# An attention layer and an RWKV block in one pipeline: mixing products in pairs of row groups, additions moved to VectorE, and the FFN shift made on ScalarE

## The reference, cut to what matters

```
def _block(x, state, ...):
    xa = _ln(x, ln1_w, ln1_b)
    sx = concatenate([state[:, 1:2] - xa[:, :1], xa[:, :-1] - xa[:, 1:]], axis=1)
    xxx = tanh((xa + sx * maa_x) @ maa_w1).reshape(b, l, 5, DM)      # DM = 32
    xxx = einsum('blfd,fde->blfe', xxx, maa_w2)
    xm = xa[:, :, None] + sx[:, :, None] * (maa_stack + xxx)
    xk, xw, xv, xr, xg = (xm[:, :, j] for j in range(5))
    w = exp(-exp(time_decay + tanh(xw @ td_w1) @ td_w2))             # DD = 64
    r, k, v = xr @ Wr.T, xk @ Wk.T, xv @ Wv.T
    g = silu(xg @ Wg.T)
    # recurrence over time, per head of 16:  out = r.(u*k v + s);  s = k v + w*s
    og = group_norm(out) * gn_w + gn_b
    x1 = x + og * g @ Wo.T
    xc = _ln(x1, ln2_w, ln2_b)
    sx2 = concatenate([state[:, 0:1] - xc[:, :1], xc[:, :-1] - xc[:, 1:]], axis=1)
    xk2 = xc + sx2 * ffn_maa_k
    xr2 = xc + sx2 * ffn_maa_r
    return x1 + sigmoid(xr2 @ Wfr.T) * (square(relu(xk2 @ Wfk.T)) @ Wfv.T)
```

## Time and profile before

| | |
|---|---|
| median of 3 runs | 2310.33 us (2305.45 to 2311.19) |
| the profiled execution | 2308.37 us |
| its span, first to last instruction | 2306.2 us |
| mean granted TensorE clock | 0.953 |
| HBM traffic | 77 GB/s over the span |

### The profile page before, as it was taken

How to read it: one execution, slowest core, us unless ns; L and a number is a source line. 1 busy time by engine, 2 the same in 40 slices (tenths; PEclk the granted TensorE clock), 3 DMA queues, 4 the chain that set the end, 5 groups by cost and what they waited for, 6 DMA issues and landing times. The chain is left out here.

```text
span 2306.2 us, 34734 instructions
## 1 busy us (share of the span) xinstructions
PE 1971.5 (85%) x12548; PEld 1364.5 (59%) x12548; DVE 1993.5 (86%) x2788; ACT 904.6 (39%) x1793; POOL 1118.4 (48%) x818
## 2 busy tenths in 40 slices
PE   6778898889898889899889889888889888999746
PEld 3556665556666556666555666555666555666624
DVE  3698899988999898899898989998898998899872
ACT  3334434344433443434444443434443334444111
POOL 1344555454555554455545455545455555445431
PEclk8999999999999999999999999999999999999877
DMA  5232232222232232232222223222223222222220
GB/s 199 76 86 83 79 88 78 82 78 81 83 91 79 80 83 79 78 89 78 82 81 79 85 82 88 79 81 77 83 82 87 80 81 83 76 76 81 78 60 9
DMA packets 86136, 189.17 MB, mean 82 GB/s; under 512 B 18800, under 2 KB 35312, under 8 KB 84944
## 3 DMA queue, kind: packets, MB, share of 16 engines
q1 hardware_dynamic: 64464, 170.19, 25.8%
q10 hardware_dynamic: 21504, 16.78, 2.4%
HBM read 161.78 MB, written 16.78 MB: 77 GB/s over the span
## 5 line engine op out<-in xcount | busy, mean ns | idle before, releaser
L605 DVE TENSOR_TENSOR_SCAN S<-wrep,S 128x1024 f32<-128x1024 f32 x256 | 605.8, 2366 | 3.4
L430 POOL TENSOR_TENSOR xf<-xf,xa 128x512 f32<-128x512 f32 x160 | 321.9, 2012 | 285.5 <-DVE xf L570 281.1
L446 POOL COPY S<-s 128x8 f32<-128x8 f32 x256 | 283.5, 1108 | 310.2 <-PE bank L1071 276.7
L614 DVE TENSOR_TENSOR S<-S,rT 128x1024 f32<-128x1024 f32 x256 | 363.3, 1419 | 3.4
L596 DVE TENSOR_TENSOR S<-vrep,kT 128x1016 f32<-128x1016 f32 x256 | 341.5, 1334 | 0.0
L400 POOL TENSOR_SCALAR rstd<-mv 128x1 f32<-128x1 f32 (+1 forms) x96 | 102.3, 1066 | 489.5 <-DVE mv L534 302.1
L1071 PE MATMUL bank<-S,slide 128*32 128x256 f32 x2048 | 176.1, 418 | 130.5 <-DVE S L614 130.5
L570 DVE SCALAR_TENSOR_TENSOR xf<-bank,par,sx 128x128 f32<-128x128 f32 x640 | 179.1, 341 | 59.2 <-PE bank L1031 56.4
L957 PE MATMUL bank<-xf,Wk 128*128 128x128 f32 x1024 | 128.4, 286 | 66.9 <-ACT prob L778 63.6
L402 POOL TENSOR_TENSOR hrs<-hrs,mhalf 128x32 f32<-128x32 f32 x32 | 175.5, 5486 | 2.7
L1071 PEld LDWEIGHTS bank<-S,slide 128*32 128x32 f32 x2048 | 41.5, 111 | 224.0 <-DVE S L614 161.7
(11 more groups left out here) (124 smaller groups left out, 3607.1 us busy)
## 6 DMA issues: line engine op xcount, KB each, us to landing
vrep<-v_dram SPq DMA_DIRECT2D x256, 512.0 KB
xc<-x_c SPq DMA_DIRECT2D x32, 256.0 KB, 2.6
xs<-x_s SPq DMA_DIRECT2D x32, 256.0 KB, 3.0
xres<-xin SPq DMA_DIRECT2D x32, 256.0 KB, 2.4
v_dram<-vT ACTq DMA_DIRECT2D x32, 256.0 KB, 2.3
out<-rr ACTq DMA_DIRECT2D x32, 256.0 KB, 2.9
Wv<-big_w SPq DMA_DIRECT2D x1, 1024.0 KB, 8.2
Wk<-big_w SPq DMA_DIRECT2D x1, 1024.0 KB, 10.0
```

The source lines that it names most:

```text
L430: po.tensor_tensor(xf[:, b, :, :], xf[:, b, :, :], xa[:, :, 1:P + 1], ALU.add).then_inc(pool_mid.sem, 1)
L446: po.tensor_copy(S[:, u % 2, :, 0], s0[:, p, k:k + UJ]).then_inc(pool_wkv.sem, 1)
L605: ve_.tensor_tensor_scan(s, wrep[:, u % C, :, :].rearrange("p j t -> p (j t)"), s, 0.0, ALU.mult, ALU.add).then_inc(dve_wkv.sem, 1)
L614: ve_.tensor_tensor(s, s, rT[:, p, u % C, :].unsqueeze(1).broadcast_to([P, UJ, P]), ALU.mult).then_inc(dve_wkv.sem, 1)
```

## The change

Three edits at once.

1. Mixing products in pairs. `mid_M` takes two factors and alternates between them, so that neighbouring products use different groups of 32 rows and different banks: `v` with `w`, `k` with `r`; `g` stays alone. `Mr` moves ahead of `Vp`. The decay's second product is made in two groups of 64 rows as well: `D1` now makes its result twice (128 columns of weights rather than 64), and `D2` and a new job `E2` share the four chunks. The lists of banks change with it: `Vp` takes the bank of `S2`, `D1` that of `S3`, `Kp` that of `Mk`.
2. The additions of `xa` to `xf` and the last residual addition go from GpSimd to VectorE, each right behind the instructions that it needs. The mixing of `r` moves from behind outer product 5 to ahead of read 4 on VectorE.
3. The FFN shift as two halves: GpSimd computes from the parameters, once, `prev` = ln2 * mix and `here` = ln2 - prev; ScalarE makes from the transposed row, in 16 activations, `xk2` and `xr2` with `here` and `xp2` (one column later) with `prev`; VectorE adds the two with one instruction for each of `xk2` and `xr2`. All eight activations for `xk2` come before those for `xr2`.

```
-    "Tx:mid Mn:att Mm:att V:att W1:mid S0:att S1:att Mv:mid Mw:mid S2:att S3:att Mk:mid Vp:mid D1:mid "
-    "Kp:mid Mr:mid D2:mid T0:att T1:att T2:att T3:att Mg:mid Rp:mid O:att G:mid").split())]
+    "Tx:mid Mn:att Mm:att V:att W1:mid S0:att S1:att Mv:mid Mw:mid S2:att S3:att Mk:mid Mr:mid Vp:mid "
+    "D1:mid Kp:mid D2:mid E2:mid T0:att T1:att T2:att T3:att Mg:mid Rp:mid O:att G:mid").split())]
...
# GpSimd, once
+            ln = par[:, COLS["ln2_w"]:COLS["ln2_w"] + 2 * C].rearrange("p (k c) -> p k c", k=2)
+            for i, name in enumerate(("ffn_maa_k", "ffn_maa_r")):
+                mix = par[:, COLS[name]:COLS[name] + C].unsqueeze(1).broadcast_to([P, 2, C])
+                po.tensor_tensor(prev[:, i, :, :], ln, mix, ALU.mult).then_inc(pool_const, 1)
+            eng.wait_ge(pool_const, 12)
+            for i in range(2):
+                po.tensor_tensor(here[:, i, :, :], ln, prev[:, i, :, :], ALU.subtract).then_inc(pool_const, 1)
...
# GpSimd, each step
-            def mid_add(n, m, p, i):
-                f, b = ORDER[i], i % 3
-                eng.wait_ge(dve_mid.sem, dve_mid.count(f"m{f}", n))
-                po.tensor_tensor(xf[:, b, :, :], xf[:, b, :, :], xa[:, :, 1:P + 1],
-                                 ALU.add).then_inc(pool_mid.sem, 1)
...
-                po.tensor_copy(xc2[:, :, 0], st0[:, p, :]).then_inc(pool_tail.sem, 1)
-            def fin_out(n, m, p):
-                eng.wait_ge(dve_fin.sem, dve_fin.count("y", n))
-                po.tensor_tensor(rr[:, :], rr[:, :], x1[:, :], ALU.add).then_inc(pool_fin.sem, 1)
+                po.tensor_tensor(xp2[:, :, :, 0], st0[:, p, :].unsqueeze(1).broadcast_to([P, 2, C]), mix,
+                                 ALU.mult).then_inc(pool_tail.sem, 1)
...
# VectorE, mid_mix
                 last.then_inc(dve_mid.sem, 1)
+                eng.wait_ge(dve_mid.sem, dve_mid.count(f"m{f}", n))
+                ve_.tensor_tensor(xf[:, b, :, :], xf[:, b, :, :], xa[:, :, 1:P + 1],
+                                  ALU.add).then_inc(dve_mid.sem, 1)
...
# VectorE, tail_shift becomes tail_mix
-                ve_.tensor_tensor(sx2[:, :, :], xc2[:, :, 0:P], xc2[:, :, 1:P + 1],
-                                  ALU.subtract).then_inc(dve_tail.sem, 1)
...
-                for dst, mix in ((xk2, "ffn_maa_k"), (xr2, "ffn_maa_r")):
-                    for c in range(C):
-                        last = ve_.scalar_tensor_tensor(dst[:, c, :], sx2[:, c, :], col(mix, c), xc2[:, c, 1:P + 1],
-                                                        ALU.mult, ALU.add)
-                    last.then_inc(dve_tail.sem, 1)
+                for i, (dst, label) in enumerate(((xk2, "xk"), (xr2, "xr"))):
+                    eng.wait_ge(act_tail.sem, act_tail.count(label, n))
+                    ve_.tensor_tensor(dst[:, :, :], dst[:, :, :], xp2[:, i, :, 0:P], ALU.add).then_inc(dve_tail.sem, 1)
...
# VectorE, fin_y
+                eng.wait_ge(dve_fin.sem, dve_fin.count("y", n))
+                ve_.tensor_tensor(rr[:, :], rr[:, :], x1[:, :], ALU.add).then_inc(dve_fin.sem, 1)
...
# ScalarE, tail_xc2
-                for c in range(C):
-                    last = sc.activation(xc2[:, c, 1:P + 1], bank_of("Tx2")[:, c * P:(c + 1) * P], ACT.Identity,
-                                         bias=col("ln2_b", c), scale=col("ln2_w", c))
-                last.then_inc(act_tail.sem, 1)
+                eng.wait_ge(pe_fin.sem, pe_fin.count("FR", n - 1))
+                for i, dst in enumerate((xk2, xr2)):
+                    for c in range(C):
+                        ps = bank_of("Tx2")[:, c * P:(c + 1) * P]
+                        sc.activation(dst[:, c, :], ps, ACT.Identity,
+                                      bias=here[:, i, 1, c:c + 1], scale=here[:, i, 0, c:c + 1])
+                        last = sc.activation(xp2[:, i, c, 1:P + 1], ps, ACT.Identity,
+                                             bias=prev[:, i, 1, c:c + 1], scale=prev[:, i, 0, c:c + 1])
+                    last.then_inc(act_tail.sem, 1)
...
# TensorE, mid_M
+            def mid_M(n, m, p, fs):
+                eng.wait_ge(act_mid.sem, act_mid.count("tx", n))
+                for f in fs:
+                    eng.wait_ge(*bank_free(f"M{f}", n))
+                for c in range(C):
+                    for f in fs:
+                        i = MIX.index(f)
+                        w, x_ = (w2g[:, :], txg[:, :]) if f == "g" else \
+                            (w2[DM * i:DM * i + DM, :], tx[DM * i:DM * i + DM, :])
+                        last = pe.matmul(bank_of(f"M{f}")[:, c * P:(c + 1) * P], w[:, c * P:(c + 1) * P], x_,
+                                         start=True, stop=True)
+                        if c == C - 1:
+                            last.then_inc(pe_mid.sem, 1)
...
# TensorE, mid_D2
-                for c in range(C):
-                    last = pe.matmul(bank_of("D2")[:, c * P:(c + 1) * P], tw2[:, c * P:(c + 1) * P], dt[:, :],
+                eng.wait_ge(*bank_free("E2", n))
+                for c in range(2):
+                    pe.matmul(bank_of("D2")[:, c * P:(c + 1) * P], tw2[0:DD, c, :], dt[0:DD, :],
+                              start=True, stop=True)
+                    last = pe.matmul(bank_of("E2")[:, c * P:(c + 1) * P], tw2[DD:P, c, :], dt[DD:P, :],
                                      start=True, stop=True)
...
# TensorE, the order of a step
-                if m: mid_M(*m, "v")
+                if m: mid_M(*m, "vw")
                 if w: wkv_sum(*w, 2)
-                if m: mid_M(*m, "w")
                 if a: att_S(*a, 2)
                 if a: att_S(*a, 3)
-                if m: mid_M(*m, "k")
+                if m: mid_M(*m, "kr")
                 if t: tail_Tg(*t)
                 if m: mid_P(*m, "v", "Vp", "Wv")
                 if w: wkv_sum(*w, 3)
                 if m: mid_D1(*m)
                 if m: mid_P(*m, "k", "Kp", "Wk")
-                if m: mid_M(*m, "r")
```

More of the change, by code:

```diff
@@ L31 @@
 U = C * HS // UJ
-CONSTS = 10 + C
+CONSTS = 14 + C
 LAG = {"att": 0, "mid": 1, "wkv": 2, "tail": 3, "fin": 4}
@@ L118, in build @@
         gnh = sb("gnh", [P, 2, C])
+        here = sb("here", [P, 2, 2, C])
+        prev = sb("prev", [P, 2, 2, C])
         W = {name: sb(name, [P, C, E]) for name in BIG}
@@ L175, in build @@
         nmr2 = sb("nmr2", [P, 1])
-        xc2 = sb("xc2", [P, C, P + 1])
-        sx2 = sb("sx2", [P, C, P])
+        xp2 = sb("xp2", [P, 2, C, P + 1])
         xr2 = sb("xr2", [P, C, P])
@@ L217, in build @@
         dve_att = Steps(sem("dve_att"), "stats aggr nm mx0 mx1 ri0 ri1 mx2 mx3 ri2 ri3 xin xst xag nm1")
-        dve_mid = Steps(sem("dve_mid"), "sx xx mv mw mk mr mg g s0m s0c")
+        dve_mid = Steps(sem("dve_mid"), "sx xx mv fv mw fw mk fk mr fr mg fg g s0m s0c")
         dve_wkv = Steps(sem("dve_wkv"), units("a s q"))
-        dve_tail = Steps(sem("dve_tail"), "o1 var o3 og x1 st ag nm sx2 xk2 xr2")
-        dve_fin = Steps(sem("dve_fin"), "y")
+        dve_tail = Steps(sem("dve_tail"), "o1 var o3 og x1 st ag nm xk2 xr2")
+        dve_fin = Steps(sem("dve_fin"), "y out")
         act_att = Steps(sem("act_att"), "xn yn Mn Mm v p0 p1 n0 n1 p2 p3 n2 n3 T0 T1 T2 T3 xhat")
@@ L224, in build @@
         act_decay = Steps(sem("act_decay"), "w0 w1 w2 w3")
-        act_tail = Steps(sem("act_tail"), "o4 sq oT xh xc2")
+        act_tail = Steps(sem("act_tail"), "o4 sq oT xh xk xr")
         act_fin = Steps(sem("act_fin"), "kr kk thr rr")
         pool_att = Steps(sem("pool_att"), "ve rs ve1 rs1")
-        pool_mid = Steps(sem("pool_mid"), "xa0 fv fw fk fr fg")
+        pool_mid = Steps(sem("pool_mid"), "xa0")
         pool_wkv = Steps(sem("pool_wkv"), "z0 z1 rk z2 z3 z4 z5 z6 z7")
         pool_tail = Steps(sem("pool_tail"), "hve hrs ve rs xc20")
-        pool_fin = Steps(sem("pool_fin"), "out")
         pe_att = Steps(sem("pe_att"), "Mn Mm V S0 S1 S2 S3 T0 T1 T2 T3 O")
-        pe_mid = Steps(sem("pe_mid"), "Tx W1 Mv Mw Mk Vp D1 Kp Mr D2 Mg Rp G")
+        pe_mid = Steps(sem("pe_mid"), "Tx W1 Mv Mw Mk Mr Vp D1 Kp D2 Mg Rp G")
         pe_wkv = Steps(sem("pe_wkv"), units("r"))
@@ L817, in mid_dt @@
                 eng.wait_ge(pe_mid.sem, pe_mid.count("D1", n))
-                sc.activation(dt[:, :], bank_of("D1")[0:DD, 0:P], ACT.Tanh).then_inc(act_mid.sem, 1)
+                sc.activation(dt[:, :], bank_of("D1")[:, 0:P], ACT.Tanh).then_inc(act_mid.sem, 1)
             def mid_k(n, m, p):
@@ L828, in mid_ez @@
                 for c in range(C):
-                    last = sc.activation(ez[:, c, :], bank_of("D2")[:, c * P:(c + 1) * P], ACT.Exp,
+                    ps = bank_of("D2" if c < 2 else "E2")
+                    last = sc.activation(ez[:, c, :], ps[:, c % 2 * P:(c % 2 + 1) * P], ACT.Exp,
                                          bias=col("time_decay", c))
@@ L896, in fin_store @@
             def fin_store(n, m, p):
-                eng.wait_ge(pool_fin.sem, pool_fin.count("out", n))
+                eng.wait_ge(dve_fin.sem, dve_fin.count("out", n))
```

55 lines of the change are left out of this document (18 added, 37 removed).

## The result

The changed kernel takes 2393.26 us (median of 4 runs, 2391.82 to 2393.61), the kernel before 2309.84 (4 runs, 2305.45 to 2311.19): a ratio of 1.0369, 95% interval 1.0354 to 1.0384, so slower by 3.7%. The predicted 2375 was 18 us short; the measured time lies inside the prediction's range of 2308 to 2412, and 0.3 us above the upper end of the forecast's own, 2353 to 2393. The profiled run took 2393.61, with a span of 2391.9 and a mean granted clock of 0.916; before, the span was 2306.2 and the clock 0.953.

A forecast was written before the change was run, and what follows sets the result against it. Two loops of near-equal length: VectorE's own work, and its maxima through ScalarE and TensorE to its FFN shift. The latter gave 70.63 us a step: 2.2 over 29 steps, plus 4, made 2378, leaned to 2375 us; range 2308 to 2412.

The forecast's parts named there:

- Steps 1 and 2: Two additions delay max2 and its exponential to m + 8.88; Vp, on S2's bank, starts at 9.81, not 6.41.
- Step 3: ScalarE in order: vT 3.78 us after Vp's start, two DMA issues 1.55 more, so tile 3's exponential starts at 15.14.
- Step 4: On TensorE, D1 takes S3's bank and starts at m + 16.07, where Kp started at 13.91.
- Step 5: TensorE from D1 to Tx2: 17.18 us without a gap, 0.10 less for split D2; Tx2 starts at m + 33.15.
- Step 6: ScalarE starts 1.63 us after Tx2; sixteen activations 0.347 apart take 5.66, ending at m + 40.44.
- Step 7: VectorE's last shift addition follows ScalarE, the read 0.65 later at m + 41.09; about 2.2 us of waiting.
- Row groups: Paired mixing products on TensorE: loads mostly one after another, so Mv 0.5 us later at m; split D2 0.1 less.
- row groups run together: Rival: TensorE's row groups do overlap; step 69.6 us, total 2349; chance 0.12.
- the clock once more: Rival: TensorE's granted clock falls a second time, at Vp; 1.2 us taken, step 71.8, total 2412; chance 0.09.
- VectorE's own sum: VectorE's work per step: 4.26 added, 1.56 removed, 3.26 of GpSimd hold-ups given back; net -0.56 us.
- The clock falls in no step: Rival: TensorE's once-a-step clock fall at the head sum's gap never comes; step 69.0 us, total 2332; chance 0.12.
- VectorE's balance decides: Rival: ScalarE's xr is ready by m + 38.2, so VectorE's work sets the step, 67.86; about 2298; chance 0.16.

The follow-up runs named there:

- a_fill: The changed kernel with unread products in TensorE's four gaps (before the first head sum, S3, Vp and D1): 2293.16 us, ratio 0.9929 to the kernel before.
- p2_fill_all: `p2_only` with unread products in all its gaps (before the first head sum, S3, Vp and Kp): 2306.38 us, ratio 1.0015 to the kernel before.
- a_fill_S3: The changed kernel with two unread products in the gap before S3 only: 2396.27 us, ratio 1.0379 to the kernel before.
- p2_fill: `p2_only` with unread products before the first head sum (three) and before Kp (two): 2371.66 us, ratio 1.0265 to the kernel before.
- p2_only: The kernel before with only the additions moved from GpSimd to VectorE, old lists of banks: 2394.2 us, ratio 1.0374.
- max2_early: The changed kernel with VectorE's reciprocal 1 and maximum 2 ahead of scan 3: 2330.8 us, ratio 1.0088 to the kernel before.
- p3_only: The kernel before with only the FFN shift made in two halves: 2303.97 us, ratio 0.999.

## Why the prediction was right, and where it was not

The direction, the place and the range were right; the forecast's step of 70.63 was 0.9 to 1.1 short, as the net of a term that was left out of the sum and two that were taken too high. The ordinary step of 71.49 us, against the prediction's own steps:

- *Steps 1 and 2.* `Vp` starts at m + 9.82 (1181.11); predicted 9.81. The exponential of S2 releases it.
- *Step 3.* vT follows the start of `Vp` by 5.57 us, not 3.78, since `Vp` runs at the lower clock. The two DMA issues end with the start of exp3, at m + 16.99 instead of 15.14.
- *Step 4.* `D1` starts at m + 17.91 (1189.20) instead of 16.07. **This 1.84 is the size that was missing**, and nearly all of it is the clock: a second fall was a rival with a chance of 0.09 and a price of 1.2.
- *Step 5.* From `D1` to `Tx2` are 16.55 us (1189.20 to 1205.75), not 17.08: `D2` in two row groups runs fully together, 0.65 us from the start of its first instruction to that of `Wo`, where it was 1.08 before and the prediction took off only 0.10. That is 0.33 of the 0.53; the rest is `D1` in 0.96 where `Mr` took 1.08, and `Kp` in 3.67 instead of 3.74.
- *Step 6.* From `Tx2` to the second addition are 7.36 us, reckoned 1.63 + 5.66 = 7.29; the sixteen activations keep a pace of 0.343. The 0.29 that the prediction set beside its row is for an activation with one operand in memory; these have two, scale and bias, and the earlier trace rows show the difference: four with both take 1.50 us, four with bias alone 1.14.
- *Step 7.* That addition starts at m + 41.82, reckoned 40.44: 1.84 - 0.53 + 0.07 = 1.38. The wait ahead of it is 1.27, and 1.33 shows at `Wo`, where 2.2 in all was reckoned. From the read (1213.72) to the next m are 29.06, reckoned 29.04.
- *Row groups.* `Mv` is not late. The pair takes 1.16 us, as the product of 8 did, and the wait at m stays 1.25. The 0.5 was wrong, and so was its reason:

```profile
1170.10 0.97 PEld L1027 LDWEIGHTS bank<-tx,w 32*128 32x128 f32 x16 [0.76 <-issue]
```

The row is of the first pair, `v` with `w`. Sixteen loads of 187 ns would need 3.0 us one after the other, 1.6 by the estimate of 0.1 us of transfer each; they were done in 0.97. The rival "row groups run together" (chance 0.12) was right as a mechanism, and so was the rule in the Trainium skill ("TensorEngine Tiling (Array Packing)", Theoretical Speedup), which the prediction had weighed less than its own slope of two rows. The trace agrees for two groups of 32 rows; no run here has four.

Together: 70.63 + 1.38 - 0.5, and 0.02 less for the rest, is 71.49. The two rivals that the prediction held apart, row groups together (-1.0) and the clock once more (here +1.84), both came, and their prices partly cancelled. That 2375 lies only 18 us off is luck in part, here and in the time outside the full steps (below). The fourth step, with its longer fall, brings the mean to 71.69.

VectorE's own sum held. The reads, outer products and scans are at 1.223, 1.211 and 2.292 us over the whole run, as said; an addition lasts 0.69, and it costs the overlap with its forerunner besides, as reckoned. The balance that this leaves, 67.86 a step, was never reached: the best kernel without a fall has 67.66, but with its order changed, and the changed order itself 68.07. The time outside the 29 steps was put at +4 and came to about -6: the 27 steps measured make 85.5 of the 85.7, and 29 at their mean would be 92. This hid another 10 us of the steps' error. (The 2290 that the prediction gives for VectorE's balance with the bound of the additions doesn't follow from its terms: 29 x -1.2 + 4 is -31, 2279.)

*The other rivals.* "The clock falls in no step" had a chance of 0.12; the filled kernel shows what it would have been, 68.07 a step, which is 0.9 below the 69.0 reckoned for it since the row groups run together too. "VectorE's balance decides" failed as it was said to, at the wait for ScalarE. "Nothing to see" needed both gains together; `a_fill` is that case, and even a little faster than before (0.7%).

**The step that failed** is therefore the sentence that gaps of 2.17 us "did not cause one in this step". It was true of the one step read, but not of the whole trace. In the kernel before, `Kp` is slow in two steps of 27 (of 70.99 and 69.93 us, where the quiet ones have 68.3 to 68.5), and `Vp` in one more (5.11, in a step of 68.90):

```profile
930.67 5.44 PE L957 MATMUL bank<-xf,Wk 128*128 128x128 f32 x32 [3.09 <-ACT prob L778]
...
1752.23 5.44 PE L957 MATMUL bank<-xf,Wk 128*128 128x128 f32 x32 [2.28 <-ACT prob L778]
```

The second has a gap hardly longer than the 2.17 to 2.26 us at which `Kp` kept its clock in the others, so a chance of 0.09 was too low by the prediction's own trace. The prediction also left out the gap before S3, which grew from 1.14 to 2.95 us: TensorE comes to it 1.08 us earlier, since the pair takes the time of one product, and the exponential that it waits for is 0.73 later. The change thus put three gaps close together (2.95, 2.05 and 1.99 us here), with 32-row products between the first two, and the clock fell. That the loss goes when the clock stays up is shown (`a_fill`, `p2_fill_all`). Which combination of gaps and of work between them brings the fall is only partly shown: the gap before S3 is not needed for it (`a_fill_S3`), and it can move from `Kp` ahead to S3 and `Vp` when others are filled (`p2_fill`). Filling the gap before `Vp` alone was not tried. Why an order with six more additions on VectorE, and no new bank, falls at `Kp` in two thirds of its steps while the kernel before seldom does, stays open beyond its gap of 2.73 instead of 2.17.

## What to carry to other kernels

An edit that only makes TensorE wait a little longer can cost far more than the wait, if its granted clock falls there: look at the granted clock around each gap, in every step of the trace and not in one, and price the work behind them at both levels, with a good chance for the worse one. What a fall costs depends on what waits behind it: one fall a step cost the old order next to nothing (68.28 us with it and without), two cost the new one 3.4. Before judging such an edit, fill the gaps with products that nobody reads; if the time jumps, the loss is the clock's, and the filling may stay as the remedy. Then follow each wait that an improvement removes to the next one: here 1.1 us taken away at the wait for `Mv` came back at `hrs`, and four fifths of what left the wait for `xr` at `C`.

## What the runs showed of the hardware that was not expected

- Products of 32 rows in two row groups overlap fully, their weight loads too: 16 instructions in 1.16 us, where 8 in one group took 1.15.
- A kernel with a period can settle into a pattern of falls: `p2_only` repeated 71.67 or 71.68 us for the last 16 of its full steps, `a_fill` 68.07; the changed kernel repeats a pattern of four steps, `max2_early` of three. A step then gets longer by a whole second fall, from 0.4 us (`p3_only`, at `Vp`) to 2.8 (`max2_early`), not in proportion to the edit.
- Some 2.7 us of unread products (6 instructions, two for each product) in one gap of 3.29 left the head sum only 0.71 us of gap, and with the three other gaps filled as well the clock stayed at full level through the step. More work on TensorE made the changed kernel 100 us faster.
- The kernel before paid next to nothing for a fall in each step. With two gaps filled it is 0.35% faster, and its steps are 68.28; most of the 0.24 us between this and its mean of 68.52 is in the three steps with a second fall (70.99, 69.93 and 68.90).
